# Moving the key product of the next batch to the end of a step in a fused audio tower (convolution, attention, quantized feed-forward)

## The reference, cut to what matters

```python
h = tok(x)                          # x: 16 batches x 256 frames x 128; 5-frame window -> 252 rows x 256,
                                    # linear, relu, affine with running statistics
y = layernorm(h)
q, k, v = y @ Wq, y @ Wk, y @ Wv    # 16 heads of 16
sim = q @ k.T * 16**-0.5 + rel_bias # causal mask
h = h + softmax(sim) @ v @ Wo + bo
h = h + ffn(layernorm(h))           # gate/up/down, 4-bit weights, 16-bit activations, scales over the whole tensor
```

## Time and profile before

| what | value |
|---|---|
| time, median of 3 runs | 849.69 us (849.53 to 849.99) |
| profiled execution | 851.06 us, span 849.2 us, mean granted PE clock 0.893 |
| PE busy | 621.2 us (73% of the span) |
| DVE busy | 619.2 us (73%) |
| ACT busy | 430.2 us (51%) |
| steps of the first stage | about 26.2 us each in the loop |
| DMA `q_st<-qh`, `k_st<-kh` | 32 each, 128 KB, median 4.0 us from issue to landing |

### The profile page before, as it was taken

The page is one execution under the profiler, slowest core; times in us unless marked ns, Lnnn a source line. Parts: engine busy times, 40 slices in busy tenths (PEclk is TensorE's granted clock), DMA queues, the critical chain, the costliest instruction groups (busy, mean ns, idle before and its releaser), DMA issues. The chain is left out here.

```text
span 849.2 us, 15260 instructions
## 1 busy us (share of the span) xinstructions
PE 621.2 (73%) x5130; PEld 464.5 (55%) x5130; DVE 619.2 (73%) x965; ACT 430.2 (51%) x622; POOL 182.2 (21%) x228
## 2 busy tenths in 40 slices
PE   2625789898999988998989886299997720002998
PEld 1224577777777777777777654144443310002998
DVE  5656777898888888888988763346579996995442
ACT  0501434664446654466544553144498872444772
POOL 1121221122211222212222000000036552550000
PEclk9976999999999999999999975599999975555999
DMA  6233022221333312333122200000033312661343
GB/s 178 89 124 44 11 35 46 57 47 29 50 44 56 54 29 41 47 53 56 32 38 51 39 13 13 13 0 0 0 147 154 158 53 73 218 220 49 113 133 97
DMA packets 40063, 57.37 MB, mean 68 GB/s; under 512 B 5820, under 2 KB 31868, under 8 KB 40028
## 3 DMA queue, kind: packets, MB, share of 16 engines
q1 hardware_dynamic: 38876, 56.13, 26.2%
q10 hardware_dynamic: 1152, 0.79, 0.4%
HBM read 25.06 MB, written 19.13 MB: 52 GB/s over the span
## 5 line engine op out<-in xcount | busy, mean ns | idle before, releaser
L724 DVE TENSOR_REDUCE mx<-ps 126x2 f32<-126x504 f32 (+1 forms) x192 | 124.6, 674 | 44.4 <-PE ps L585 44.0
L1376 PE MATMUL ps<-wdT,oh 128*126 128x256 f16 x384 | 66.2, 280 | 92.7 <-DVE ol L1336 92.7
L807 ACT ACTIVATE pt<-sbr 126x504 f32<-126x504 f32 x192 | 114.8, 617 | 26.1 <-DVE sbr L715 24.9
L715 DVE TENSOR_TENSOR sbr<-ps,biasT 126x504 f32<-126x504 f32 x192 | 120.0, 675 | 8.9 <-PE ps L603 8.4
L1376 PEld LDWEIGHTS ps<-wdT,oh 128*126 128x126 f16 x384 | 48.9, 140 | 93.5 <-DVE ol L1336 93.5
L582 PE MATMUL ps<-biasN,identb 126*126 126x504 bf16 x192 | 75.8, 395 | 25.6 <-DMA k_st<-kl 25.6
L880 POOL TENSOR_TENSOR h<-h,bc 126x512 f32<-126x512 f32 x16 | 20.2, 1266 | 291.0 <-ACT h L821 291.0
L585 PE MATMUL ps<-k_st,q_st 65*126 65x252 f16 (+1 forms) x512 | 76.2, 252 | 0.0
L1047 PE MATMUL ps<-x2t,wgT 128*128 (+1 forms) x288 | 63.7, 386 | 11.0 <-DVE x2t L1090 11.0
L1047 PE MATMUL ps<-x2t,wuT 128*128 (+1 forms) x288 | 63.4, 376 | 11.1 <-ACT raw L1216 11.0
L585 PEld LDWEIGHTS ps<-k_st,q_st 65*126 65x126 f16 x512 | 61.5, 142 | 16.2 <-issue 1.9
(11 more groups left out here) (174 smaller groups left out, 1428.7 us busy)
## 6 DMA issues: line engine op xcount, KB each, us to landing
up_raw<-raw SPq DMA_DIRECT2D x14, 756.0 KB, 3.2
raw<-up_raw SPq DMA_DIRECT2D x14, 756.0 KB, 4.4
q_st<-qh SPq DMA_DIRECT2D x32, 128.0 KB, 4.0
k_st<-kh SPq DMA_DIRECT2D x32, 128.0 KB, 4.0
res<-hall SPq DMA_DIRECT2D x16, 252.0 KB
hin<-res SPq DMA_DIRECT2D x16, 252.0 KB
out<-y SPq DMA_DIRECT2D x16, 252.0 KB
xin<-in_x SPq DMA_DIRECT2D x16, 128.0 KB, 3.6
```

The source lines that it names most:

```text
L715: nc.vector.tensor_tensor(sbr[0:TT, n % 4].rearrange("p (h w) -> p h w", w=w), ps[0:TT, score_bank[name, n], 0:2 * N].rearrange("p (h w) - ...
L724: nc.vector.tensor_reduce(mx[0:TT, 0 if w == TT else 1, heads[0]:heads[-1] + 1], ps[0:TT, score_bank[name, n], 0:2 * N].rearrange("p (h w) ...
L807: nc.scalar.activation(pt[0:TT, n // 3 % 2, n % 3], sbr[0:TT, n % 4], ACT.Exp).then_inc(S["exp_r"], 1)
L1376: last = nc.tensor.matmul(ps[0:TT, s, t * C:(t + 1) * C], o[par][:, m, rows], wdT[:, w, m], start=(m == 0 and i == 0), stop=(m == MT - 1 a ...
```

## The change

The key product of batch b+2 goes from the start of step b+1 to the end of step b, between P2[10] and P2[11]; both parts of the queries go in front of P2[9]. `kh` and `kl` follow on ACT and DVE ahead of P2[11]'s own work; `ax` and `osb(0, 2)` go behind it. In the ring of banks `k` becomes the last, behind `x2T` of the same step. SP's list is the same.

```diff
-        PE_ORDER = [P2[0], ("k", 1, 0), ("k", 1, 1), P2[1], ("conv", 2, 0), ("PV", -1, 3), P2[2], P2[3],
+        PE_ORDER = [P2[0], P2[1], ("conv", 2, 0), ("PV", -1, 3), P2[2], P2[3],
...
-                    P2[6], P2[7], P2[8], ("mT", 1, 0), ("q", 2, 0), P2[9], ("x2T", -1, 0), P2[10], ("q", 2, 1),
-                    P2[11], ("PV", 0, 2)]
-        DVE_ORDER = [P2[0], P2[1], ("kl", 1), P2[2], P2[3], P2[4], P2[5], ("on", -1, 0), P1[0], ("on", -1, 1),
+                    P2[6], P2[7], P2[8], ("mT", 1, 0), ("q", 2, 0), ("q", 2, 1), P2[9], ("x2T", -1, 0), P2[10],
+                    ("k", 2, 0), ("k", 2, 1), P2[11], ("PV", 0, 2)]
+        DVE_ORDER = [P2[0], P2[1], P2[2], P2[3], P2[4], P2[5], ("on", -1, 0), P1[0], ("on", -1, 1),
...
-                     ("xnl", 2), P2[6], P2[7], P2[8], P2[9], P2[10], ("ax", -1), ("ql", 2), P2[11]]
-        ACT_ORDER = [P2[0], ("kh", 1), P2[1], ("osb", -1, 3), P2[2], P2[3], P2[4], P2[5], ("osb", 0, 0),
+                     ("xnl", 2), P2[6], P2[7], P2[8], P2[9], P2[10], ("ql", 2), ("kl", 2), P2[11],
+                     ("ax", -1)]
+        ACT_ORDER = [P2[0], P2[1], ("osb", -1, 3), P2[2], P2[3], P2[4], P2[5], ("osb", 0, 0),
...
-                     P2[6], ("mneg", 1), P2[7], P2[8], ("x2", -1), P2[9], ("qh", 2), P2[10], ("osb", 0, 2), P2[11]]
+                     P2[6], ("mneg", 1), P2[7], P2[8], ("x2", -1), P2[9], ("qh", 2), P2[10], ("kh", 2), P2[11],
+                     ("osb", 0, 2)]
...
-                  (-2, ("xnl", 2)): [("ffdq", 0, 1)], (-1, ("kl", 1)): [("ffdq", 0, 2), ("ffpow", 0)]}
+                  (-2, ("xnl", 2)): [("ffdq", 0, 1)], (-2, ("kl", 2)): [("ffdq", 0, 2), ("ffpow", 0)]}
...
-                [("k", "kl_r", 1, 1, 1), ("OT0", "on_r", 2, 1, -1), ("OT1", "on_r", 2, 2, -1),
+                [("OT0", "on_r", 2, 1, -1), ("OT1", "on_r", 2, 2, -1),
                  ("onT", "onl_r", 1, 1, -1), ("wo", "h2_r", 1, 1, -1), ("xT", "xl_r", 1, 1, 3),
-                 ("mT", "mneg_r", 1, 1, 1), ("x2T", "x2_r", 1, 1, -1)]]
+                 ("mT", "mneg_r", 1, 1, 1), ("x2T", "x2_r", 1, 1, -1), ("k", "kl_r", 1, 1, 2)]]
```

## The result

The changed kernel takes 859.56 us (median of 6 runs, 855.53 to 860.73) against 849.84 us for the kernel before (6 runs, 848.40 to 853.48): ratio 1.0088, interval 1.0065 to 1.0111. That is +9.7 us by the medians and +7.5 by the ratio (849.84 x 0.0088), where +6.2 was forecast; the time lies in the range, and the direction is the forecast one. The profiled execution took 859.84 us (span 858.0, mean granted PE clock 0.899), 8.8 us more than the one before.

What follows compares the result with a forecast made beforehand. Bound: a loop through P1[0]'s wait for the last key copy. Steps 4 to 14 +7.0 us, steps 2 and 3 +0.4, step 1 -0.5, end -0.7: +6.2 us, 855.9 us against the median 849.69; range 846 to 861.

Steps and rivals of the forecast that it cites:

- The hole and the queries: Steady step, PE: q's second half (0.65 us) fills x2T's 0.47 us hold; x2T starts at about 313.06 rather than 313.04.
- The keys behind `x2`: Steady step, PE: k must wait until ACT has read x2T's bank, a new wait of 0.80 us (bounds 0 and 1.1).
- The first issue behind P2[11]: Steady step, SP: the first query copy waits for P2[11] instead of qh and is issued 0.78 us later.
- Six copies in a row: Steady step: first issue to P1[0] takes 8.75 us, before 8.89 (bounds 7.4 and 8.98); P1[0] starts 0.64 us later.
- Steps 1 to 3: Early steps: step 1 wins 0.5 us, steps 2 and 3 lose 0.2 us each.
- PV behind the exponential: Start of the next step, PE: PV of group 3 newly waits 0.9 us, covered by the wait for the copies.
- The end: End of the stage: with osb behind it the last exponential starts sooner, 0.7 us won (bounds 0 to 1.0).
- PE's clock in the loop: Rival, steady steps: PE's clock falls to its lower level in part of each step, 869 us; chance 0.07.
- The queue keeps up: Rival, steady steps: six copies take 7.4 to 8.0 us, PE's own path sets P1[0], 845.9 us; chance 0.16.
- The draw: Rival, steady steps: six copies take 8.1 to 8.4 us, -2 to +2 us, 848 to 852 us; chance 0.1.

## Why the prediction was right

Every sign that it named for the steady step is there: the keys behind `x2`, the first issue on P2[11]'s end, six issues in one row, kl's landing over 5 us, PV behind the exponential, P1[0] behind kl's copy. The number is nearer than its parts, and that is luck: from the first queries to `mT` of step 14 the loss is 8.1 us where 6.9 was forecast, the end won 2.9 us where 0.7 was, and the two errors cancel in part. The stated range decides little, since it holds a gain of nearly 4 us as well.

*The hole and the queries:* as worked out. x2T has no wait, and the queries alone change nothing (ratio 1.0013).

*The keys behind `x2`:* 0.66 us where 0.80 was predicted.

*The first issue behind P2[11]:* 0.82 us later where 0.78 was predicted. Shown from both sides: with the keys behind P2[11] it comes 4.63 us after `mT` again and the step falls back to 26.2 us.

*Six copies in a row:* 8.89 us where 8.75 was predicted, too little by 0.14 us in each step. It had joined the landing of ql with three copies at 1.03 us. Both parts come out within the 0.1 us to which landings are told: ql lands 1.27 + 4.4 = 5.67 us after the first issue and kl 3.22 + 5.6 = 8.82, so the three copies take 3.15. The sum also ended at kl's landing, and P1[0] starts a little behind that. Step -1, the nearest row, gave 8.95 and was the better guide, though the prediction named it as the reason for 8.75. With that the loss per step is 0.81 instead of 0.64: first issues at 213.20 and 456.64 after, 210.56 and 446.49 before, so nine steps grew by 243.44 - 235.93 = 7.5 us, 0.83 each.

*Steps 1 to 3:* the first issues of steps 1, 2 and 3 come 1.90, 1.39 and 2.20 us later than before, the start's 1.6 us in it. So step 1 won its 0.5 us, but not by the mechanism forecast. Its six copies took 140.69 - 131.60 = 9.09 us where 8.75 was predicted and 9.25 was the time before, and the next first issue came 0.8 us later after its `mT`, as in the steady steps. What outweighs that is PE's clock. From P1[0] to `mT` in step 1, before and after:

```profile
138.95:152.58 13.63, 13.47 (x111) 11.61 (x111) 12.13 (x27) 4.31 (x10) 6.15 (x11) 0.87 0.06 21
140.69:153.16 12.47, 11.91 (x112) 10.19 (x112) 11.76 (x27) 4.20 (x10) 6.14 (x11) 1.00 0.07 23
```

In the kernel before, the granted clock is 0.87 there, behind P1[0]'s wait of 1.75 us; in the changed one, where P1[0] waits 0.62 us, it is 1.00, and the stretch is 1.16 us shorter. Steps 2 and 3 lost 1.25 us together (from the first issue of step 2 to that of step 4, 213.20 - 158.61 after and 210.56 - 157.22 before) where 0.4 was predicted.

*PV behind the exponential:* 0.74 us where 0.9 was predicted, and covered as said. How much time PE had behind that cover was mis-sized: with the copies quick, the changed order has a step of 25.91 us (128 partitions), 0.31 below before, not 0.12.

*The end:* -2.9 us where -0.7 was predicted. PV's wait for the exponential in step 16 fell from 1.01 to 0.52 us, which is the mechanism that I had named, at 0.5 us. The rest, which the prediction did not have, goes with PE's clock in the last steps: over 43 us (505 to 548) the granted clock is 0.65, and PE is busy 24.41 us with 194 instructions; before, 495.63 to 540 us, it was 0.62 and 27.90 us with the same 194. More of the stretch lies on the upper of the two levels (2.4 GHz). Why it held longer was not tried. The other versions of this stage had ends of 51.5 to 54.3 us, and with `osb` moved the end is in the main the shorter the higher the clock is over it: 51.5 to 51.7 us at 0.68 (four profiles), 53.6 to 53.8 at 0.59 (three). Without the move, and also at 0.59, it is 54.3 (the queries alone), so at the same clock the move would be worth 0.5 to 0.7 us, as forecast; that is a single comparison.

*PE's clock in the loop* stayed at 1.00 in the steady steps, so that rival fell for this change; with x2T behind the keys it came. *The queue keeps up* fell by kl's 5.6 us, and the half-sized copies show that it would have been right with quicker transfers: 2.4 to 2.5 us, no wait, faster than before. *The draw* fell with the 8.89 us.

*What is left:* the trace accounts for +5.1 us in what the change touches, the ratio for +7.5, the medians for +9.7. The interval of the ratio begins at 849.84 x 0.0065 = 5.5 us. The difference is about the variation of the untouched stretches in the profiled pair (3.7 us); that it is only this has not been shown.

## What to carry to other kernels

Where several transfers stand in line, moving the producer of a late one forward is worth nothing if the line is what takes the time: look for what releases the first of them, and what the move puts in front of that. Follow a ring of buffers and an engine's list one tenant further than the edit, since a wait moved out of one place turns up at the next (x2T behind the keys, 2.21 us; an exponential behind `qh`, 0.84 us). Here a single entry of ACT's list, `qh` ahead of `x2`, together with the keys behind P2[11], gave 1.5%.

## What the runs showed of the hardware that I had not expected

A copy of 128 KB from SBUF to SBUF in pieces of 512 B costs about 1.0 us in a row of six when it writes 16 partitions (8.82 us to the last landing with six, 7.86 with five), and a second queue made the row no shorter (9.25 us to P1[0] instead of 8.89). The layout of the destination counts for far more than issuing sooner: landing 5.6 us with 16 partitions, 4.9 with 32, 2.2 with all 128, in one run each for the last two.

PE's clock fell inside the loop in two places: after PE had stood for 2.21 us (x2T behind the keys) its granted clock was 0.50, and in step 1 of the kernel before it was 0.87 over the 13.63 us that follow a wait of 1.75 us. After the steady steps' waits of 1.19 us it stayed at 1.00.
